# A fused MLA-attention and SwiGLU layer on one core: the opening stage reordered on all engines, with its constants in one transfer and a second load queue

## The reference

```python
x = x + attn(layernorm(x))        # x: 8 batches x 512 rows x 512
x = x + ffn(layernorm(x))
# attn, 16 heads, 128 + 64 query/key columns, 128 value columns
q  = rmsnorm(x @ wq_a.T, q_norm_w) @ wq_b.T          # latent of 384
kv = x @ wkv_a.T                                     # 128 latent + 64 rotary columns
kv_c = rmsnorm(kv[..., :128], kv_norm_w); k_pe = rope(kv[..., 128:])
k_nope, v = split(kv_c @ wkv_b.T)
out = softmax((q_nope @ k_nope + rope(q_pe) @ k_pe) / sqrt(192)) @ v @ wo.T
# ffn: silu(x @ fp8(gate_w) * gate_scale) * (x @ fp8(up_w) * up_scale), then @ fp8(down_w) * down_scale
```

## Time and profile before

| | |
|---|---|
| median of three runs | 2262.19 us |
| the profiled execution, its own time | 2260.38 us |
| its span in the trace | 2258.4 us |
| PE busy | 2212.3 us (98%) |
| DVE, ACT, POOL busy | 1574.5, 1066.6, 1010.7 us |
| granted TensorE clock, mean | 0.996 |
| start of head 0's scores | 64.37 us |
| start of head 1's scores | 74.30 us |

### The profile page before, as it was taken

The page is one execution under the profiler, slowest core; times in us unless marked ns, Lnnn a source line. Parts: engine busy times, 40 slices in busy tenths (PEclk is TensorE's granted clock), DMA queues, the critical chain, the costliest instruction groups (busy, mean ns, idle before and its releaser), DMA issues.

```text
span 2258.4 us, 36337 instructions
## 1 busy us (share of the span) xinstructions
PE 2212.3 (98%) x10940; PEld 1026.4 (45%) x10940; DVE 1574.5 (70%) x3310; ACT 1066.6 (47%) x2336; POOL 1010.7 (45%) x697
## 2 busy tenths in 40 slices
PE   7999999999999999999999999999999999999988
PEld 4444544445444454444544445444454445444444
DVE  7788786777477764777648776587755877567773
ACT  4666664554345542555435553355433554345532
POOL 4657365453345533554244542436334363343322
PEclk9999999999999999999999999999999999999999
DMA  7756424452154520645116451254514454144430
GB/s 259 160 125 140 104 70 122 105 125 60 29 141 105 123 53 23 157 105 121 43 34 149 106 120 35 64 126 109 117 24 99 110 114 94 24 106 105 105 64 19
DMA packets 703831, 219.77 MB, mean 97 GB/s; under 512 B 685520, under 2 KB 685776, under 8 KB 702672
## 3 DMA queue, kind: packets, MB, share of 16 engines
q1 hardware_dynamic: 703696, 218.09, 41.5%
HBM read 40.78 MB, written 8.39 MB: 22 GB/s over the span
## 4 chain that ended last, share of the span: by engine, by line
PE 87%; DVE 7%; issue 2%; ACT 1%; DMA 1%; SPq 1%; POOL 1%; DVEq 0%; POOLq 0%; ACTq 0%
PE bank L810 13%; PE bank L283 10%; PE bank L285 10%; PE bank L284 10%; PE scores L820 7%; PE scores L621 5%; PE scores L285 5%; PE scores L284 5%; PE scores L283 5%; PE bank L632 4%; PE bank L633 4%; PE bank L634 4%; PE scores L618 3%; DVE arena L1325 2%; PE bank L797 1%
## 5 line engine op out<-in xcount | busy, mean ns | idle before, releaser
L1531 POOL TENSOR_TENSOR arena<-arena 128x1024 f16<-128x1024 f32 x256 | 545.6, 2132 | 633.9 <-ACT arena L979 633.7
L977 ACT ACTIVATE arena<-scores,shift 128x512 f32<-128x512 f32 x512 | 357.9, 699 | 560.6 <-DVE shift L1305 549.2
L1325 DVE SCALAR_TENSOR_TENSOR arena<-bank,rden,arena 128x512 f32<-128x512 f32 x512 | 350.7, 744 | 144.6 <-PE bank L285 144.6
L1303 DVE TENSOR_REDUCE mx<-scores 128x1 f32<-128x512 f32 x512 | 353.5, 690 | 12.6 <-PE scores L285 7.6
L979 ACT ACTIVATE arena<-scores,shift 128x512 f16<-128x512 f32 x512 | 359.0, 701 | 0.0
L810 PE MATMUL bank<-arena,WFF 128*128 128x512 f16 x1408 | 317.0, 379 | 3.0 <-DVE arena L1420 3.0
L1591 POOL TENSOR_TENSOR arena<-arena 128x512 f16<-128x512 f32 x96 | 114.5, 1192 | 284.5 <-ACT arena L1042 284.5
L1100 DVE SCALAR_TENSOR_TENSOR arena<-bank,arena 128x512 f16<-128x512 f32 (+1 forms) x263 | 176.5, 671 | 55.0 <-ACT arena L970 50.4
L810 PEld LDWEIGHTS bank<-arena,WFF 128*128 128x128 f16 x1408 | 137.6, 98 | 168.0 <-DVE arena L1420 4.0
L283 PE MATMUL bank<-WVO,arena 128*128 (+1 forms) x512 | 194.1, 379 | 1.5 <-DVE arena L1100 1.0
L621 PE MATMUL scores<-arena 128*128 128x512 f16 x512 | 195.4, 382 | 0.0
(11 more groups left out here) (154 smaller groups left out, 3491.8 us busy)
## 6 DMA issues: line engine op xcount, KB each, us to landing
arena<-arena SPq DMA_TRANSPOSE x712, 2.7
arena<-w_ffn SPq DMA_DIRECT2D x24, 384.0 KB, 3.4
arena<-x SPq DMA_DIRECT2D x8, 1024.0 KB, 6.3
out<-arena SPq DMA_DIRECT2D x32, 256.0 KB, 2.0
arena<-x SPq DMA_DIRECT2D x14, 512.0 KB, 3.9
WVO<-w_o SPq DMA_DIRECT2D x4, 1024.0 KB, 5.9
arena<-w_nope SPq DMA_DIRECT2D x4, 768.0 KB, 14.8
arena<-down_scale SPq DMA_DIRECT2D x8, 256.0 KB, 3.3
```

The lines of the kernel that those rows point to most:

```text
L977: act.activation(P32[:, t, :], SC[:, t, :], ACT.Exp, scale=EXP_SCALE, bias=shift[:, t:t + 1], accum_out=esum[:, par, t:t + 1]).then_inc(s[ ...
L1303: dve.tensor_reduce(mx[:, t:t + 1], SC[:, t, :], AX_X, ALU.max).then_inc(s["mxr"], 1)
L1325: dve.scalar_tensor_tensor(out=XR[:, t, :], in0=banks[t][:, :], scalar=rden[:, t:t + 1], in1=XR[:, t, :], op0=ALU.mult, op1=ALU.add).then_ ...
L1531: pool.tensor_tensor(PL[:, par, two, :], P32[:, two, :], PH[:, par, two, :], ALU.subtract).then_inc(s["pl"], 1)
```

## The change

- The five constants and the identity become one array and one transfer (`cst`), all behind `ld_const`.
- SP's queue loads x tiles 0 and 2, `cst`, `w_k`, `w_pe` (in two transfers), `w_nope`, `w_v` and `w_o`; ACT's queue loads x tiles 1 and 3 and `w_a`.
- Key latents come before query latents, on PE, ACT and DVE; `kv_hi` and `kpe_hi` stand ahead of ACT's last two query latents.
- The `w_pe` rounding is spread: parts 0 and 1 between the latents, part 2 behind them.
- DVE scales the norm columns before the `w_a` rests; the gate and up scales later.
- POOL's scaling of `w_k` waits also for the first x rounding (`xth` >= 1).
- PE: absorbed 0 to 7; rotated 0 to 3; absorb(0); absorbed 8 and 9; absorb(1); absorbed 10; scores of head 0; absorbed 11; output weights 0; rotated 4; output weights 1; absorb(2); rotated 5, 6, 7; scores of head 1.
- POOL: absorbed halves 3 and 4; rotations 0 to 3; halves 5 and 6; head 0; then halves 7, rotation 4, halves 8, rotation 5, halves 9, rotation 6, halves 10, rotation 7; head 1; halves 11.
- The staging tile has nine places in place of four; the residual x is loaded behind head 0.

```diff
@@ ab_step @@
-            dst = (BQ, BC, BT)[m][:, :] if m < N_AB_FIRST else SC[:, m % 3, :]
+            dst = (BQ[:, :], BT[:, :], BC[:, :], BO[:, :], SC[:, 0], SC[:, 1], SC[:, 2], BQ[:, :], BT[:, :], BC[:, :],
+                   BO[:, :], BT[:, :])[m]
@@ sync @@
-            for t in range(NT):
+            for t in (0, 2):
                 sp.dma_start(XN[:, t], x[0, tile(t)]).then_inc(ld_x0[t], 16)
-            sp.dma_start(ident[:], ident_d).then_inc(s["ld_id"], 16)
-            sp.dma_start(g_a, w_a).then_inc(s["ld_a"], 16)
...
+            sp.dma_start(cst[:], consts).then_inc(s["ld_const"], 16)
@@ sync, set-up @@
+            key_rows(0)
             query_rows(0, 0)
             query_rows(0, 1)
             output_matrix(1)
-            key_rows(0)
@@ tensor, absorbed_weights @@
+                if m < 7:
+                    pe.wait_ge(s["lat"], m + 1)
+                elif m < 10:
+                    pe.wait_ge(s["w_lo"], N_A + N_PE + m - 6)
                 else:
-                    pe.wait_ge(s["ab_cp"], m - N_AB_FIRST - 2)
+                    pe.wait_ge(s["ab_cp"], (1, 6)[m - 10])
@@ tensor, output_weights @@
+                if h <= 1:
+                    pe.wait_ge(s["ab_cp"], 7 + 2 * h)
@@ tensor, setup_queries_and_keys @@
-                for m in range(2 * N_AB_FIRST):
+                for m in range(8):
                     absorbed_weights(m)
...
+                pe.wait_ge(s["ab_cp"], 5)
                 absorb(0, 0)
-                absorbed_weights(6)
-                output_weights(0)
-                absorbed_weights(7)
+                absorbed_weights(8)
+                absorbed_weights(9)
                 absorb(1, 1)
-                output_weights(1)
-                for m in range(8, N_AB):
-                    absorbed_weights(m)
-                rotated(0, NT, RBANK[0])
+                absorbed_weights(10)
@@ tensor, attention @@
+                pe.wait_ge(s["kt_t"], b * 32 + 32)
                 if first:
+                    scores(b, 0, 0)
+                    absorbed_weights(11)
+                    output_weights(0)
+                    pe.wait_ge(s["ab_cp"], 8)
+                    rotated_ahead(b, NT)
+                    output_weights(1)
+                    absorb(2, base + 2)
                     pe.wait_ge(s["w_lo"], SETUP_N)
+                    rotated_ahead(b, N_ROT_FFN)
@@ scalar, setup_queries_and_keys @@
+                for i in range(NT):
+                    latent(0, i, True)
+                for j in range(2):
+                    rotation_weights_hi(j)
+                    latent(0, NT + j, True)
+                kv_hi(0)
+                kpe_hi(0)
+                latent(0, NT + 2, True)
+                latent(0, NT + 3, True)
+                rotation_weights_hi(2)
+                absorbed_hi(0)
                 for t in range(NT):
                     queries_hi(0, t)
+                absorbed_hi(1)
+                absorbed_hi(2)
+                for m in range(N_AB_FIRST, 8):
...
                     absorbed_copy(m)
+                for n in range(3):
+                    rot_hi(0, n)
...
                 qa_hi(0, 0)
+                absorbed_copy(8)
                 rot_hi(0, 3)
+                absorbed_copy(9)
                 qa_hi(1, 1)
+                absorbed_copy(10)
@@ scalar, attention @@
                 probs(base, 0, True)
+                if first:
+                    absorbed_copy(11)
+                    output_hi(0)
+                    rot_hi(0, NT)
+                    output_hi(1)
                 qa_hi(base + 2, 0)
@@ scalar, start @@
+            for t in (1, 3):
+                act.dma_start(XN[:, t], x[0, tile(t)]).then_inc(ld_x0[t], 16)
+            act.dma_start(g_a, w_a).then_inc(s["ld_a"], 16)
@@ vector, setup_queries_and_keys @@
+                setup_roots(1)
+                rotation_weights_lo(0)
+                rotation_weights_lo(1)
+                keys_lo(0)
                 setup_roots(0)
                 for t in range(NT):
                     queries_lo(0, t)
+                rotation_weights_lo(2)
                 for m in range(N_AB_FIRST):
                     absorbed_lo(m)
...
+                for n in range(NT):
+                    rot_products(0, n, SC[:, (n + 3) % NT, :])
                 rot_lo(0, 0)
                 rot_lo(0, 1)
                 qa_lo(0, 0)
                 rot_lo(0, 2)
                 rot_lo(0, 3)
@@ vector, attention @@
                 if first:
+                    maxima(base)
+                    output_lo(0)
+                    rot_products(0, NT, RBANK[0])
+                    output_lo(1)
                     rot_lo(0, NT)
+                    rot_products(b, N_ROT_FFN, RBANK[N_ROT_FFN % 2])
@@ gpsimd, attention @@
-                if first:
-                    pool.wait_ge(s["ab_lo"], 7)
-                rotate(b, N_ROT_FFN)
+                if not first:
+                    rotate(b, N_ROT_FFN)
...
+                    if first and i == 0:
+                        for n in range(NT, N_ROT):
+                            absorbed_halves(n + 3)
+                            rotate(b, n)
@@ gpsimd, set-up @@
             pool.wait_ge(s["ld_k"], 32)
+            pool.wait_ge(s["xth"], 1)
             pool.tensor_tensor(g_k, g_k, g_kn.unsqueeze(1).broadcast_to((P, NH, KL)), ALU.mult).then_inc(s["k_scaled"], 1)
```

More of the change, by code:

```diff
@@ L87, with build @@
 RMS_N = RSQRT_OPS + 1
-def build(nc, x, w_a, w_pe, w_nope, w_k, w_v, w_o, norm_cols, kv_norm_row, w_ffn,
-          gate_scale, up_scale, down_scale, ident_d, cos_d, sin_d, out):
+def build(nc, x, w_a, w_pe, w_nope, w_k, w_v, w_o, kv_norm_row, w_ffn, down_scale, consts, out):
     ctx = ExitStack()
@@ L291, in latents_order @@
         def latents_order(setup):
-            return [(w, t) for w in "qk" for t in range(NT)] if setup else LATENTS
+            return [(w, t) for w in "kq" for t in range(NT)] if setup else LATENTS
         def GBANK(c):
@@ L549, in setup_latents @@
                     pe.wait_ge(s["xtl"], t + 1)
+                    latent("k", t, True)
+                for t in range(NT):
                     latent("q", t, True)
-                for t in range(NT):
-                    latent("k", t, True)
             def rotated(a, n, dst):
@@ L845, in batch @@
                 ffn(b, last, first)
[L847 removed]
+            pe.wait_ge(s["ld_const"], 16)
             for t in range(NT):
@@ L956, in setup_queries_and_keys @@
                 qa_hi(0, 0)
-                absorbed_copy(6)
-                rot_hi(0, 2)
-                output_hi(0)
-                absorbed_copy(7)
+                absorbed_copy(8)
                 rot_hi(0, 3)
+                absorbed_copy(9)
                 qa_hi(1, 1)
-                output_hi(1)
-                for m in range(8, N_AB):
-                    absorbed_copy(m)
-                rot_hi(0, 4)
+                absorbed_copy(10)
             def qa_hi(g, par):
@@ L1051, in small_work @@
                         kv_hi(b + 1)
+                if first:
+                    act.wait_ge(s["c_cols"], 4)
                 for c in range(NF):
@@ L1081, in _ @@
             x_hi(0)
-            act.wait_ge(s["ld_pe"], 16)
-            act.wait_ge(s["c_cols"], 4)
-            for j in range(N_PE):
-                act.activation(WPE[:, 0, j, :], g_pe[:, j, :], ACT.Copy,
-                               scale=ncol[:, j:j + 1]).then_inc(s["w_hi"], 1)
-                latent(0, j, True)
-            for i in range(N_PE, 2 * NT):
-                latent(0, i, True)
             setup_queries_and_keys()
@@ L1473, in _ @@
             layer_norm(XN, XN, 0)
+            dve.wait_ge(s["ld_const"], 16)
+            cc = Chain(dve, "c_cols", 0)
+            cc.add(dve.tensor_scalar(ncol[:, 0:NQ], ncol[:, 0:NQ], WS, None, ALU.mult))
+            cc.add(dve.tensor_scalar(ncol[:, NQ:NQ + 1], ncol[:, NQ:NQ + 1], VS, None, ALU.mult))
+            cc.wait()
             for k in range(N_A):
@@ L1476, in _ @@
             x_lo(0)
-            dve.wait_ge(s["ld_const"], 16 * 5)
-            cc = Chain(dve, "c_cols", 0)
-            cc.add(dve.tensor_scalar(ncol[:, 0:NQ], ncol[:, 0:NQ], WS, None, ALU.mult))
-            cc.add(dve.tensor_scalar(ncol[:, NQ:NQ + 1], ncol[:, NQ:NQ + 1], VS, None, ALU.mult))
-            cc.add(dve.scalar_tensor_tensor(out=usc[:], in0=usc[:], scalar=FS / (2 * XS * XS), in1=gsc[:],
-                                            op0=ALU.mult, op1=ALU.mult))
-            cc.wait()
-            cc.link(dve.tensor_scalar(gsc[:], gsc[:], 0.5 / XS, None, ALU.mult))
-            for j in range(N_PE):
-                weights_lo(N_A + j, g_pe[:, j, :], lambda p, j=j: WPE[:, p, j, :], ncol[:, j:j + 1])
             setup_queries_and_keys()
@@ L1527, in head @@
                 for half in range(2):
+                    if isinstance(g, int) and g == 0 and half == 1:
+                        pool.wait_ge(s["ab_psum"], N_AB)
                     two = slice(2 * half, 2 * half + 2)
```

161 lines of the change are left out of this document (74 added, 87 removed).

## The result

| | before | after |
|---|---|---|
| median, same chip | 2261.93 us (4 runs, 2260.6 to 2262.83) | 2278.13 us (4 runs, 2269.6 to 2279.24) |
| the profiled execution, its span | 2260.38, 2258.4 us | 2269.6, 2268.0 us |
| ratio, 95% interval | | 1.0064 [1.0051, 1.0076] |

Over all its runs the changed kernel is slower by 0.64% (14.5 us by the ratio, 16.2 by the two medians), against +5.2 us forecast, and its median lies 7 us above the upper end of the range. Its profiled execution is the quickest of its four, so the profile shows only 9.6 us of the difference (2268.0 - 2258.4), and a second question is why four executions of one program lie nearly 10 us apart. The page's head and its lines on the transfers come first.

What follows compares the result with a forecast made beforehand. PE, busy 98%, bounds the kernel. Head 1's scores 2.7 us later, less 0.25, gave +2.45; a 2.7 us clock fall made +5.2: profiled 2265.6, median forecast 2267.4. Range 2256.5 to 2271, likeliest case 2265.2 to 2269.7.

Steps and rivals of the forecast that it cites:

- rival C: Set-up: POOL's w_k scaling gets in front of DVE's last w_a rest, first latent 3.5 us later; chance 0.13.
- A: The forecast case: the summed waits and a clock fall in the fourth wait, before rotated 5; +5.2 us, chance 0.40.
- Start: PE's start: x lands 1.0 us sooner, PE starts at 9.45, w_a lands at 10.3, first latent at 14.3.
- Latents: PE's latents: take 13.87 us as before, slow clock included, so PE leaves them at 28.1.
- Before absorbed 7: First new wait: PE idles 2.3 us (1.8 to 3.2) for DVE's rest of absorbed group 0.
- Before absorb(1): Second wait: PE idles 2.5 us (2.0 to 3.2) for DVE's rest of absorb(0).
- Head 0's scores: Third wait: PE idles 1.15 us for rotation 3 and head 0's rotary rows; scores start at 55.75.
- Output weights 1: PE waits 0.6 us for ACT's copy of absorbed 11, which stands behind head 0's exponentials.
- Rotated 5: Fourth wait or gap: PE idles 4.2 us (3.5 to 5) behind POOL's head 0, halves 7, rotation 4, then ACT and DVE.
- S: Start time of head 0's scores on PE, forecast 55.75 us; the later waits are counted from it.
- Rival B: The same waits, but the clock stays up behind the fourth wait, before rotated 5: +2.45 us, 2264.6; chance 0.28.
- rival D: Not slower: waits before absorbed 7 and absorb(1) mostly absent, together under 2.4 us; -3.5 us, 2258.7; chance 0.19.

Runs made afterwards that it cites:

- f2: Kernel before, with 32 unused bytes ahead of the arena (base 119072); median 2265.53 us, ratio 1.0014 to the kernel before.
- g3: Kernel before, with the arena moved by 64 bytes (base 119104); median 2264.33 us, ratio 1.0015 to the kernel before.
- h1: Kernel before, with the arena moved by 128 bytes (base 119168); median 2264.55 us, ratio 1.0014 to the kernel before.
- h2: Kernel before, with the arena moved by 256 bytes (base 119296); median 2261.8 us, ratio 1.0002 to the kernel before.
- h3: Kernel before, with the arena moved by 512 bytes (base 119552); median 2261.19 us, ratio 0.9999 to the kernel before.
- g1: Changed kernel with the arena back at 119040 and POOL's w_k scaling waiting for all four w_a rests; 2267.6 us, ratio 1.003 to the kernel before.
- e0: Changed kernel run again, unedited; median 2273.34 us, ratio 1.0055 to the kernel before.
- f1: Changed kernel with 32 unused bytes putting the arena back at 119040; median 2272.27 us, ratio 1.0044 to the kernel before.
- e1: Changed kernel with all loads on SP's queue; median 2275.09 us, ratio 1.0072 to the kernel before.
- f4: g1 plus ACT rounding output weights 1 before rot_hi of rotation 4, and DVE's rest of rotation 0 before its fourth rotary products; 2264.34 us, ratio 1.0013.
- e2: Kernel before, with x tiles 1 and 3 and w_a loaded on ACT's queue; median 2261.1 us, ratio 0.9995 to the kernel before.
- g2: f4 plus kpe_hi behind ACT's last two query latents and DVE's absorbed group 0 rest before the third w_pe rest; 2259.63 us, ratio 0.9993.
- e3: e1 plus ACT rounding output weights 1 before rotation 4's hi half; median 2270.03 us, ratio 1.0053 to the kernel before.
- f3: Changed kernel with POOL's w_k scaling waiting for all four w_a rests; median 2272.31 us, ratio 1.0045 to the kernel before.

## Why the prediction was wrong

**The step that failed** is a sentence of its first paragraph, "from there on both kernels do the same", said again of the differences after head 1's scores, "where I expect none above 0.5 us". The profiled loop is 4.8 us longer. The instructions are the same; their addresses are not. The diff replaces six small arrays by one, and whatever is allocated behind them moves, by 32 bytes. That is worth 0.5 us on each transpose and 3.2 to 3.4 us by the ratio on the whole (f2, g3, h1, against h2 and h3, which cost nothing that can be told). No chance was given to it. The second thing that put the median above the range is rival C, which had a chance and half its price. The forecast on the order alone held (g1: 2267.6).

**Rival C was right in kind and wrong in two numbers.** It had a chance of 0.13; it happened in e0's profiled execution, and, by the bunches of f1, in about half of the runs with the old gate (its share in the first four was only argued from their times). It was said to be decided by whether ACT has `w_a` before about 10.0. In e0 ACT had it at 9.43, but in f1 at 9.88, without the rest being caught. The rows show that DVE's rests began at 11.5 in any case and that POOL's start, set by the landing of `w_k` (13.08 in e0, 13.59 in f1, 13.79 in the change's profile), decides. It was priced at 3.5 us; the rest itself lost 4.3, the first latent came 4.2 later (19.33 against 15.10), and the profiled time was 7.7 above the other's. What lies between 4.2 and 7.7 is mostly clock: its falls in the stretches from 14 to 84 come to 6.73 us against 3.42, part of it in idle time, and the latents, begun at a pitch of 1.2 GHz, took 13.39 us against 11.75. The 7.06 for 2.77 us agree with the rule of the Trainium skill cited for it (SBUF — State Buffer, "Who interferes with whom"). The bound on top of A was 2270.9; three runs of four lay at 2277.5 to 2279.2, which is about what A, C at its real price (7.7) and the address (3.3) make together, 2278.4; none of the three was profiled.

**The sum to head 1's scores: +4.95 for +5.4**, term by term.

- Start: 10.19 for 9.45. A gain of 0.28 us (0.4 from e1 to e0), not 1.0; the bound "nothing" was the nearer one. `w_a` at 10.60 for 10.3, first latent 15.10 for 14.3.
- Latents: 11.75 us (15.10 to 26.85), not 13.87. The step "slow clock included; I keep that" failed: the rows at 15.10 and 15.18 are 0.08 us apart for 192 columns, 2.4 GHz from the first, where before the first four microseconds ran at 1.2. That is 2.1 us in the change's favour, and an accident of these two executions: f4's latents start at a pitch of 0.16, and those of the kernel before run at the full pitch from the first in e2, f2, g3 and h3 and at half in h1 and h2.
- Before absorbed 7: 3.49 for 2.3. The chain was right. ACT stood 1.95 us for POOL's key rotation, which the prediction named and did not add up:

```profile
22.34 3.80 POOL L1542 TENSOR_TENSOR arena<-arena,cst 128x128 f32<-128x128 f32 x4 [3.62 <-DVE rs_s L1255]
```

```profile
27.22 0.72 ACT L945 ACTIVATE arena<-arena 128x256 f16<-128x256 f32 x2 [1.95 <-POOLq L1548]
```

  Four multiplies took 3.80 us, while DVE was at its `w_pe` rests; one like operation behind them (L1545) took 0.45, and the same four in the kernel before 1.8 (33.08 to 34.80), with DVE at work on small operations. That DVE's rests held them up is likely, but was not tried. g2, which takes the key rotation out of that chain, has 1.52.
- Before absorb(1): 2.22 for 2.5. Head 0's scores: no wait of their own, since the clock stretched absorb(1) and absorbed 10 (51.63 to 56.25, 4.6 us for 2.85 of work at full clock); they start at 56.25 for 55.75. With the clock up at this place the wait is there, 0.80 us in f1 and 0.89 in e1, for 1.15.
- Output weights 1: 0.39 for 0.6. Rotated 5: 4.05 for 4.2, by the chain that was named, and at S + 15.38 for S + 15.35.
- The waits come to 21.6 for 21.3, 6.0 above before (15.57). The clock's falls behind the latents cost 0.5 us more than before, since 0.5 of the old one lay in idle time; forecast was 0 (one lost, one won back), with one fall behind the fourth gap, where there were two, of half the length. 6.0 + 0.5 - 2.1 is 4.4. Of the 0.55 left some 0.3 is how waits are counted: from the end of a matmul of 0.38 us, where the pitch is 0.22, so that each costs 0.16 more than its bracket says, and behind the latents there are two more of them than before. The rest is open.
- The 0.25 us wait for head 0's probabilities is gone, as forecast, and head 1's stand on time: between 72 and 130 us PE has one wait, of 0.20, which is there before too (124.38 and 120.03).

So the sum was close to its number by luck in part: its misses, +0.8 in the waits and the clock and -2.1 in the latents, stand against each other. From the end of the latents to head 1's scores the change takes 52.4 us for 45.3, 7.1 more. One pair of profiles also says less than two decimals do: in the profiles of the kernel before with another queue or arena place head 1's scores start at 71.69 to 74.47. g1's runs bear the size out at the median, +6.8 for +5.2. Rival B fell (the clock did fall), and rival D too, by 5.7 us in its first two waits where it needed under 2.4.

## What to carry to other kernels

A diff that adds, removes or joins arrays moves every array allocated behind it: before costing its instructions, compare the base addresses of the buffers that transfers use most, and keep those that are transposed on a multiple of 256 bytes. Where a Pool operation of several microseconds may start inside a row of Vector ones with two SBUF inputs, gate it on the last of them and not on the first semaphore that makes it legal. This reordering freed no engine and only traded waits: its three long ones were chains through a single bank and other engines, and a price read off one wait was not what its removal gave. Swapping two lines on ACT took away 3.9 us of wait, of which 1.35 came back behind it. And before a change of some microseconds is read from a pair of profiles, look at how far profiles of one kernel lie apart.

## What the runs showed of the hardware that was not expected

Transposes within SBUF are 0.5 us slower at the median (3.2 for 2.7 us), and hold the DMA engines 47.2 to 48.7% of the span for 41.5 to 42.1%, when the array they work on starts off a 256-byte multiple. A Pool operation that gets in front of a Vector one with two SBUF inputs holds it until it is over (7.06 for 2.77 us in e0), and four small Pool operations beside Vector's `w_pe` rests took 3.80 us, where one behind them took 0.45 (the cause of this second one was not tried alone). And the clock of PE's first work is not fixed for a kernel: with the same waits before it (10.1 and 1.25 us) the latents ran at the pitch of 2.4 GHz from the first in the change and g1, and at that of 1.2 GHz for their first 4.3 us in f4, which took 2.1 us more; the fall behind a wait of 2.2 us came in the change, e0, e3, f3 and g1 and not in e1 and f1. Steps of 2 us are large enough for a good part of the 4 us by which runs of one program differ here, but only one execution of each was profiled, so this is not shown.
